# A transformer layer in float32 on one core: attention and last stage in one block, the first maxima between the projections' products, and loads spread over attention

## The chip, the core and the metric

The kernel runs on one core of one Trainium2 chip. A core has five engines that each work through a queue of their own in order and wait for each other by semaphores: TensorE (PE; its weight loads are shown as PEld), VectorE (DVE), ScalarE (ACT), GpSimd (POOL) and SyncE (SP), which here only issues DMAs (SPq in the rows). The metric is the device time of one execution in microseconds (us), the median of several.

## The reference

The layer is pre-normed attention, then a pre-normed linear map whose inputs and weights are rounded to a six bit grid, each with a residual. x is 4 x 2048 x 512, with 16 heads of 32.

```python
x = x + attn(layernorm(x))
#  q = x@Wq.T + bq + ocr_bias, k = x@Wk.T + bk, v = x@Wv.T + bv
#  scores = q k^T / sqrt(32) + 0.1 for |i-j| <= 2; softmax; (attn v) @ Wo.T + bo
x = x + ffn(layernorm(x))
#  xd, wd: x and weight in blocks of 32, scaled by max/7.5, rounded to the e2m3 grid, scaled back
#  xd @ wd.T + bias
```

## The kernel before

The 8192 tokens are 16 chunks of 512 (`NCH`; `CH` = 512 tokens, `TT` = 4 tiles of 128, `KB` = 4 blocks of the 512 features). Float32 products are made of three passes on parts: hi times hi, hi times lo, lo times hi. There are three blocks, one after the other; between two of them all engines meet, so that nothing of a later block is issued before the earlier one has ended.

**Projections** (`project`, L109). For each chunk PE turns the normed chunk (16 transposes into `ps_t`), ACT takes the high part `x_hi` (L346) and DVE the low part `x_lo` (L294), and PE makes `NP` = 12 groups of 12 products (`products`, L389 to L405) into the four banks of `ps_p`: four groups each for q, k and v. ACT and DVE take them out again as high and low parts (L354, L309) or with the bias added (v, L319), and SyncE stores them to HBM (L216, L217, L220). POOL makes `xb` = x + bo (L172). At its start ACT waits for `bias_ready` ahead of all of its first chunk. The parts of the two later weights, `wo` and `wd`, are made in the first chunk and stored.

**Attention** (`attend`, L421). A unit is one group of four heads and 512 queries (`NU` = 64 units; four units share their keys). A unit has `KT` = 16 steps s of 128 keys. In each step and for each of four heads PE makes one product of scores into `ps_s` (L644), which ACT takes out with the exponential into `p_sb` (L714); DVE multiplies by the band where it is near (L751); in each second step PE weighs the values (`weigh`, L658) and POOL adds two steps' `p_sb` to a `pair` (L798), whose sums are merged by DMAs that add, on POOL's queue (L803, `join` L784). The exponential needs each query's maximum ahead of its unit. So between the scores of a unit PE makes the products of the *next* unit (`maximum`, L625, `MAXES` = 64 for a unit) into `ps_m`, DVE reduces each to a maximum (`take`, L724), and the row of them is turned and put by a DMA (`put_shift`) into the 97th row of that unit's queries. Unit 0 has no unit ahead of it: at the head of attention PE makes 64 maxima for it and 16 (`HG * LEAD`) of unit 1, with nothing between them.

**Last stage** (`finish`, L810), for each chunk c: `load_o` loads the unscaled attention output `o_raw` and the inverted sums `o_rec`, which are rows of 512 numbers that are each spread to 32 partitions; POOL scales (L912), ACT takes `o_hi` (`o_highs`, L941), POOL makes `o_lo` (L916), PE multiplies by `wo` (`out_project`, L1054), DVE adds `xb` to get `x1` and its moments (`residual`, `norm_factors`), ACT normalises (`normalise`: `std` L930 and `y` L934), DVE quantises to `xd` (`quantise`), PE turns it and multiplies by `wd` (`linear`, L1081), and DVE adds `x1` to get `res` (`last_sum`, L1007). `last_sum(c)` is dealt out between the steps of `quantise(c + 1)`, so DVE comes to it behind the normalising of the next chunk. The FFN's bias comes in as one product of 2 rows ahead of each tile (L1073). The chunks are software-pipelined by hand. The loops that set the order are:

```python
# SyncE
for c in range(NCH):
    if c + 2 < NCH: load_xb(c + 2)
    if c + 4 < NCH: load_o(c + 4)
    store(c)
# ScalarE
for c in range(NCH):
    high(c)
    if c + 1 < NCH: normalise(c + 1)
    if c + 3 < NCH: o_highs(c + 3)
```

## Time and profile before

| | us |
|---|---|
| median of 3 runs | 4258.18 (4256.25 to 4260.35) |
| profiled execution | 4247.55, with a span of 4245.8 |
| PE busy in the span | 4096.3 (96%) |
| DVE busy | 3324.0 (78%) |
| POOL busy | 3055.4 (72%) |
| ACT busy | 2406.2 (57%) |

The page has also the span in 40 slices. PE is busy for 8 tenths or more of each of them but one, the slice from 3715 to 3821 us, where it is 4. That slice holds the border between attention and the last stage; the border between projections and attention lies around 600 us. A row of a timeline has the start, the length, the engine, the line, the work with what it writes and reads, and in brackets how long the engine had been idle ahead of it and what released it. Times in the rows are those of the profiled execution, counted from its span's start.

### The profile page before, as it was taken

Reading aid. Unit: us, or ns where it says so; the run is one execution under the profiler, and the core shown is the slowest. Engines: PE = TensorE matmul, PEld = TensorE weight load, DVE = VectorE, ACT = ScalarE, POOL = GpSimd, SP = SyncE. Lnnn points to the kernel's source line nnn. Section 1 sums busy time; section 2 is a strip of 40 time slices with the busy share of each in tenths; the row PEclk is TensorE's granted clock in tenths of the full one; section 3 lists DMA queues with packets and bytes.
Section 4 is the critical chain, followed back from the end, with each engine's and each line's share of the span. In section 5 each row is a group of like instructions: output and inputs, shape, how many; then the busy total and the mean of one; then the engine's idle time right before and its main releaser. Section 6 shows DMA issues by size and latency. Waiting matters only on the chain. (4 is left out here: it accounts for less than half of the span.)

```text
span 4245.8 us, 60060 instructions
## 1 busy us (share of the span) xinstructions
PE 4096.3 (96%) x21392; PEld 2549.3 (60%) x21392; DVE 3324.0 (78%) x5623; ACT 2406.2 (57%) x4652; POOL 3055.4 (72%) x1111
## 2 busy tenths in 40 slices
PE   8999989999999999999999999999999999949999
PEld 6888855555555555555555555555555555417777
DVE  5444449888888888888888888888888888617776
ACT  2222215766766677667666676666766677623221
POOL 2111116888889898989989889888888888935552
PEclk9999988999999999999999999999999999969999
DMA  7666655899999999999999999998999999775442
GB/s 267 207 207 207 207 173 122 182 211 190 202 197 193 201 193 208 187 206 186 212 191 196 198 192 208 186 210 184 210 190 199 195 193 188 160 185 177 160 160 72
DMA packets 283849, 808.30 MB, mean 190 GB/s; under 512 B 28609, under 2 KB 95169, under 8 KB 221122
## 3 DMA queue, kind: packets, MB, share of 16 engines
q0 software_dynamic: 64512, 469.79, 55.7%
q1 hardware_dynamic: 219074, 335.10, 27.1%
q8 instruction: 153, 2.51, 0.2%
q14 instruction: 110, 0.90, 0.1%
HBM read 195.04 MB, written 139.46 MB: 79 GB/s over the span
## 5 line engine op out<-in xcount | busy, mean ns | idle before, releaser
L724 DVE TENSOR_REDUCE part_max<-ps_m 128x1 f32<-128x512 f32 x4096 | 2512.3, 678 | 383.6 <-PE ps_m L625 383.3
L798 POOL TENSOR_TENSOR pair<-p_sb 128x2048 f32<-128x2048 f32 x512 | 2458.1, 4823 | 104.4 <-DVE p_sb L751 58.6
L714 ACT ACTIVATE p_sb<-ps_s 128x512 f32<-128x512 f32 x4096 | 2083.3, 614 | 769.6 <-PE ps_s L644 765.7
L644 PE MATMUL ps_s<-q_st,k_st 97*128 97x512 f32 x4096 | 1687.4, 413 | 6.1 <-DMA q_st<-shift 4.1
L625 PE MATMUL ps_m<-k_st,q_st 96*128 96x512 f32 x4096 | 1643.5, 405 | 20.3 <-POOL k_st L778 20.1
L644 PEld LDWEIGHTS ps_s<-q_st,k_st 97*128 97x128 f32 x4096 | 772.9, 189 | 653.8 <-issue 426.4
L658 PE MATMUL ps_o<-p_sb,v_sb 128*32 128x512 f32 x8192 | 993.4, 602 | 31.2 <-DVE p_sb L751 18.8
L625 PEld LDWEIGHTS ps_m<-k_st,q_st 96*128 96x128 f32 x4096 | 787.3, 192 | 190.9 <-DVE part_max L724 37.6
L658 PEld LDWEIGHTS ps_o<-p_sb,v_sb 128*32 128x32 f32 x8192 | 224.1, 109 | 512.2 <-ACT p_sb L714 320.9
L803 POOL DMA_DIRECT2D pair<-pair x384 | 336.2, 875 | 218.0 <-POOL pair L798 172.5
L172 POOL TENSOR_TENSOR xb<-xin,bo_row 128x2048 f32<-128x2048 f32 x16 | 73.8, 4613 | 418.3 <-DMA xin<-in_x 407.6
L751 DVE TENSOR_TENSOR p_sb<-p_sb,band_f 128x520 f32<-128x520 f32 (+2 forms) x352 | 219.1, 650 | 47.1 <-ACT p_sb L714 47.1
L309 DVE SCALAR_TENSOR_TENSOR s_lo<-ps_p,bias,s_hi 128x512 fp32r<-128x512 f32 x128 | 96.0, 750 | 172.0 <-ACT s_hi L354 172.0
L354 ACT ACTIVATE s_hi<-ps_p,bias 128x512 fp32r<-128x512 f32 x128 | 88.2, 689 | 245.5 <-PE ps_p L405 237.3
L916 POOL TENSOR_TENSOR o_lo<-o_raw,o_hi 128x512 fp32r<-128x512 f32 x60 | 128.1, 2163 | 134.3 <-ACT o_hi L941 134.3
L405 PE MATMUL ps_p<-x_hi,w_hi 128*128 128x512 f32 x512 | 203.7, 398 | 8.3 <-DVE x_lo L294 8.2
L405 PE MATMUL ps_p<-x_hi,w_lo 128*128 128x512 f32 x512 | 201.4, 393 | 0.0
L405 PE MATMUL ps_p<-x_lo,w_hi 128*128 128x512 f32 x512 | 201.0, 393 | 0.0
L1054 PE MATMUL ps_r<-wo_hi,o_hi 128*128 128x512 f32 x256 | 104.1, 406 | 39.9 <-DVE o_lo L1016 26.2
L319 DVE TENSOR_TENSOR v_st<-ps_p,bv_row 128x512 f32<-128x512 f32 x64 | 44.1, 691 | 118.5 <-PE ps_p L405 118.5
L700 ACT ACTIVATE sum_st<-ps_m 128x512 f32<-128x512 f32 x64 | 38.3, 598 | 161.8 <-PE ps_m L666 161.8
L346 ACT ACTIVATE x_hi<-ps_t 128x512 fp32r<-128x512 f32 x64 | 33.0, 602 | 160.4 <-PE ps_t L379 160.4
(98 smaller groups left out, 2685.5 us busy)
## 6 DMA issues: line engine op xcount, KB each, us to landing
pair<-pair POOLq DMA_DIRECT2D x448, 1024.0 KB, 8.6
q_st<-q_hi_d SPq DMA_DIRECT2D x128, 256.0 KB, 7.3
k_st<-k_hi_d SPq DMA_DIRECT2D x128, 256.0 KB, 12.2
xin<-in_x SPq DMA_DIRECT2D x16, 1024.0 KB, 8.3
xb_d<-xb SPq DMA_DIRECT2D x16, 1024.0 KB, 5.2
q_hi_d<-s_hi SPq DMA_DIRECT2D x64, 256.0 KB, 2.1
q_lo_d<-s_lo SPq DMA_DIRECT2D x64, 256.0 KB, 2.3
k_hi_d<-s_hi SPq DMA_DIRECT2D x64, 256.0 KB, 2.3
```

Source lines behind the costliest of these rows:

```text
L309: nc.vector.scalar_tensor_tensor(out=s_lo[:, n % RING], in0=ps_p[:, n % RING], scalar=bias[:, n // NHG, n % NHG:n % NHG + 1], in1=f32(s_hi ...
L405: last = nc.tensor.matmul(ps_p[:, n % RING], lhs, rhs, start=(k == 0 and j == 0), stop=(k == KB - 1 and j == 2))
L625: nc.tensor.matmul(ps_m[:, bank, :], q_st[0:ROWS, u, h, t * P:(t + 1) * P], k_st[0:ROWS, g % 2, n, h, :], start=True, stop=True).then_inc( ...
L644: nc.tensor.matmul(ps_s[:, (HG * s + h) % RING_S, :], k_st[0:ROWS + 1, unit // QC % 2, kt // TT, h, kt % TT * P:(kt % TT + 1) * P], q_st[0 ...
L658: last = nc.tensor.matmul(ps_o[h * HD:(h + 1) * HD, :], v_sb[:, kt, h * HD:(h + 1) * HD], p_sb[:, s % SLOTS, h, :], start=(kt == 0), stop= ...
L714: nc.scalar.activation(p_sb[:, s % SLOTS, h, :], ps_s[:, (HG * s + h) % RING_S, :], ACT.Exp, scale=SCALE).then_inc(p_ready, 1)
L724: nc.vector.tensor_reduce(part_max[:, unit % 2, col, n:n + 1], ps_m[:, max_place(unit, j) % RING_M, :], AX.X, ALU.max).then_inc(max_taken, 1)
L751: nc.vector.tensor_tensor(view, view, factor, ALU.mult).then_inc(banded, 1)
L798: nc.gpsimd.tensor_tensor(pair[:, m % PAIR_RING], p_sb[:, s % SLOTS], p_sb[:, (s + 1) % SLOTS], ALU.add).then_inc(paired, 1)
L803: pool.dma_start(pair[:, m % PAIR_RING], pair[:, (m - CHAINS) % PAIR_RING], accum_op=ALU.add).then_inc(merged[n % CHAINS], 16)
L916: nc.gpsimd.tensor_tensor(o_lo[:, b, g, :], o_raw[:, b, g, :], f32(o_hi[:, b, g, :]), ALU.subtract).then_inc(o_split, 1)
L1054: last = nc.tensor.matmul(ps_r[:, t, :], lhs, rhs, start=(k == 0 and j == 0), stop=(k == NHG - 1 and j == 2))
```

## The change

- `attend` and `finish` become one block, `attend_and_finish`; the last stage's tiles lie in buffers that attention no longer needs by then (`x1` is a ring of three in `p_sb`, and the load of `xb` goes straight into `x1`).
- The 80 first maxima and the turn of unit 0's row are made in `project`, between the groups of the last three chunks: `places(c, n)` gives 22, 22 and 37 of the 81 places to the chunks, 1 to 4 behind each group. Their products go to the banks of `ps_t`, and DVE's `take` stands behind each of its own steps. The keys and queries they need are loaded in `load_first`, behind the fifth chunk. The queries are a ring of three units instead of four.
- The loads of the last stage's first chunks and of `wo` stand between the steps of attention's last units. The output projection of chunk 0 is made between the last unit's scores (`between_scores`), DVE scales chunks 0 and 1 (`scale_o`, `o_low`).
- The FFN's bias is written to the output in the projections, 1 MB with each chunk, and the last stage's result is added to it by a DMA that adds, on POOL's queue. The product L1073 is gone.
- In the first chunk ACT waits for `bias_ready` only ahead of `s_hi`, and POOL waits for the normed chunk ahead of its first `xb`.
- The loops of the last stage load later (`load_o(c + 2)` where it was `c + 4`), in another order.

```diff
+    AHEAD = MAXES + HG * LEAD + 1
+    TURN_PLACE = MAXES + TURN_AFTER
...
+    def places(c, n):
+        ends = (0, 22, 44, AHEAD)
+        i = c - (NCH - 3)
+        count = ends[i + 1] - ends[i]
+        return range(ends[i] + count * n // NP, ends[i] + count * (n + 1) // NP)
...
+            pool.wait_ge(xhat_ready, TT)
...
+            def load_first():
+                for s in part_out:
+                    sp.wait_ge(s, 64 * QC)
+                sp.wait_ge(late_out, 64)
+                for u in range(QC):
+                    for r, part in enumerate((k_hi_d, k_lo_d, k_hi_d)):
+                        sp.dma_start(f32(k_even[r * HD:(r + 1) * HD, u]),
+                                     part[u].rearrange("(h d) t -> d h t", d=HD)).then_inc(k_loaded[u], 16)
+                for u in range(2):
+                    for r, part in enumerate((q_hi_d, q_hi_d, q_lo_d)):
+                        sp.dma_start(f32(q_st[r * HD:(r + 1) * HD, u]),
+                                     part[u].rearrange("(h d) t -> d h t", d=HD)).then_inc(q_loaded[u], 16)
...
+                if last:
+                    sp.wait_ge(max_taken, TURN_PLACE + 1)
+                    sp.dma_start(f32(q_st[ROWS:ROWS + 1, 0]).rearrange("o h (t q) -> o (h t) q", q=P),
+                                 f32(shift[:])).then_inc(shift_loaded, 16)
...
+                sp.dma_start(out_ch[c], ffn_b.unsqueeze(0).unsqueeze(0).to_broadcast([P, TT, D])).then_inc(bias_out, 16)
...
-            with sp.Fori(1, NCH - 2) as c:
+            with sp.Fori(1, QC + 1) as c:
+                chunk(c, True)
+            load_first()
+            with sp.Fori(QC + 1, NCH - 2) as c:
...
+            sp.wait_ge(bias_out, 16 * NCH)
...
+            def take(c, n):
+                for place in places(c, n):
+                    v.wait_ge(max_scored, place + 1)
...
+                    unit, j = max_of(place)
+                    n_, col = j // (HG * TT), j % (HG * TT)
+                    nc.vector.tensor_reduce(part_max[:, unit, col, n_:n_ + 1], ps_t[:, place % RING_M, :],
+                                            AX.X, ALU.max).then_inc(max_taken, 1)
+                    if place == MAXES:
+                        v.wait_ge(max_taken, MAXES)
+                        nc.vector.tensor_reduce(neg_max[:], part_max[:, 0], AX.X, ALU.max, negate=True).then_inc(max_row, 1)
...
+            def ahead(c, n):
+                for place in places(c, n):
+                    at_least(pe, max_taken, place - RING_M + 1)
+                    if place == TURN_PLACE:
+                        pe.wait_ge(max_row, 1)
+                        nc.tensor.transpose(ps_t[0:HG * TT, place % RING_M, 0:P], neg_max[:], ident[:]).then_inc(max_scored, 1)
+                        continue
...
+                    nc.tensor.matmul(ps_t[:, place % RING_M, :], q_st[0:ROWS, unit, h, t * P:(t + 1) * P],
+                                     k_even[0:ROWS, n_, h, :], start=True, stop=True).then_inc(max_scored, 1)
...
+            for c in range(NCH - 3, NCH):
+                if c > NCH - 3:
+                    pe.wait_ge(max_taken, places(c, 0)[0])
+                turn(c)
+                for n in range(NP):
+                    products(c, n)
+                    ahead(c, n)
...
+        o_first = sb("o_first", [P, NHG, CH])
+        o_hi, o_lo = (k_even[:, 0], q_st[:, 1]), (q_st[:, 2], k_odd[:, 0])
+        wo_hi, wo_lo, wd_hi, wd_lo = k_even[:, 2], k_even[:, 3], k_odd[:, 1], k_odd[:, 2]
+        t_hi, t_lo = k_odd[:, 3], q_st[:, 0]
+        x1 = (p_sb[:, 4], p_sb[:, 5], p_sb[:, 0])
...
+        res = (pair[:, 2], pair[:, 3])
...
+        def o_rec(c):
+            return pair[:, 4] if c > 1 and c % 2 == 0 else f32(k_even[:, 1])
...
+        def o_raw(c):
+            return p_sb[:, 3] if c > 1 and c % 2 == 0 else o_first
...
+            def load_o(c):
+                at_least(sp, o_split, NHG * (1 if c == 1 else c - 1))
+                sp.wait_ge(o_out, 16 * ((NHG - 1) * NCH + c + 1))
+                sp.dma_start(o_raw(c)[:], o_by_chunk[c]).then_inc(o_in[c % 2], 16)
...
+            def load_rec(c, gs=range(NHG)):
+                at_least(sp, o_scaled, NHG * (1 if c == 1 else c - 1))
...
+                for g in gs:
+                    sp.dma_start(o_rec(c)[:, g, :],
+                                 rec_d[g * NCH + c].unsqueeze(1).to_broadcast([HG, HD, CH])).then_inc(rec_in[c % 2], 16)
...
+            def load_xb(c):
+                at_least(sp, res_ready, TT * (c - 2))
+                sp.dma_start(x1[c % 3], xb_d[c]).then_inc(xb_in[c % 3], 16)
...
+                    if 0 < unit < NU - 2 and kt == 1:
+                        sp.wait_ge(scored, HG * KT * unit)
+                        load_q(unit + 2)
...
+                    if unit == NU - QC and kt == 6:
+                        sp.wait_ge(scored, HG * KT * QC * (NG - 1))
+                        sp.dma_start(f32(wo_hi), wo_hi_d).then_inc(wo_in[0], 16)
...
+                    if unit == NU - 3 and kt == 7:
+                        load_o(0)
+                    if unit == NU - 2 and kt in (2, 4, 6, 8):
+                        load_rec(0, (kt // 2 - 1,))
+                    if unit == NU - 1 and kt in (1, 2, 3, 4):
+                        load_rec(1, (kt - 1,))
+                    if unit == NU - 1 and kt == 5:
+                        load_o(1)
+                    if unit == NU - 1 and kt == KT - 1:
+                        sp.wait_ge(pv_done, ST - 4)
+                        sp.wait_ge(paired, NM - 2)
+                        load_xb(0)
+            load_xb(1)
+            sp.wait_ge(scored, HG * ST)
+            sp.dma_start(f32(wd_hi), wd_hi_d).then_inc(wd_in, 16)
+            sp.dma_start(f32(wd_lo), wd_lo_d).then_inc(wd_in, 16)
+            sp.wait_ge(pv_done, ST)
+            sp.wait_ge(paired, NM)
+            load_xb(2)
+            for c in range(NCH):
+                if c + 2 < NCH:
+                    load_o(c + 2)
+                    load_rec(c + 2)
+                if c + 3 < NCH:
+                    load_xb(c + 3)
...
+            def between_scores(kt, h):
+                t, k = (kt - FIRST_OUT) // 2, (kt - FIRST_OUT) % 2 * 2 + h // 2
+                if h % 2 == 0 or not 0 <= t < TT:
+                    return
...
+                out_part(0, t, k)
...
+                        if s >= ST - KT:
+                            between_scores(s % KT, h)
...
+            act.wait_ge(paired, NM)
+            normalise(0)
+            for c in range(NCH):
+                high(c)
+                if c + 2 < NCH:
+                    o_highs(c + 2)
+                if c + 1 < NCH:
+                    normalise(c + 1)
...
+            def last_unit(kt):
+                if kt == 3:
+                    o_low(0)
+                if kt == 9:
+                    scale_o(1)
+                if kt == 12:
+                    o_low(1)
...
             def store(c):
-                sp.wait_ge(res_ready, TT * c + TT)
-                sp.dma_start(out_ch[c], res[:, c % 2]).then_inc(out_done[c % 2], 16)
...
-            for c in range(NCH):
-                if c + 2 < NCH:
-                    load_xb(c + 2)
-                if c + 4 < NCH:
-                    load_o(c + 4)
-                store(c)
...
-            for c in range(1, NCH):
+                pool.wait_ge(res_ready, TT * c + TT)
+                pool.dma_start(out_ch[c], res[c % 2], accum_op=ALU.add).then_inc(out_done[c % 2], 16)
+            for c in range(2, NCH):
...
+                if c > 2:
+                    store(c - 3)
+            for c in range(NCH - 3, NCH):
+                store(c)
```

SyncE in the last stage, before: `out_y` is the store of a chunk, `xb2`, `o_raw` and `o_rec` are the loads for later chunks.

```order
L874 DMA out_y<-res 128x4x512 [waits res_ready]
L870 DMA xb2<-xb_d 128x2048 [waits x1_ready]
L861 DMA o_raw<-o_d 128x4x512 [waits o_split]
L865 DMA o_rec<-rec_d 128x1x512 x4
L874 DMA out_y<-res 128x4x512 [waits res_ready]
```

SyncE there now; `p_sb` and `o_first` from `o_d` are `o_raw`, `k_even` from `rec_d` is `o_rec`, and `p_sb` from `xb_d` is `x1`.

```order
L724 DMA p_sb<-xb_d 128x2048 [waits res_ready]
L710 DMA o_first<-o_d 128x4x512 [waits o_out,o_split]
L719 DMA k_even<-rec_d 128x1x512 [waits rec_out,o_scaled]
L719 DMA k_even<-rec_d 128x1x512 x3
L724 DMA p_sb<-xb_d 128x2048 [waits res_ready]
```

The load that waits for `res_ready` stands now ahead of `o_raw` and `o_rec` of the same chunk, and the store has left this queue.

ScalarE in the last stage, before, one turn of its loop.

```order
L926 ACTIVATE t_hi<-ps_t2 128x512 [waits ffn_done,turned2]
L926 ACTIVATE t_hi<-ps_t2 128x512 [waits turned2] x3
L930 ACTIVATE std2<-mom2,eps2 128x4 [waits ln2_steps]
L934 ACTIVATE y<-x1,nmr,rstd2 128x512 [waits quant,rstd2_ready]
L934 ACTIVATE y<-x1,nmr,rstd2 128x512 x3
L941 ACTIVATE o_hi2<-o_raw 128x512 [waits o_scaled,out_projected]
L941 ACTIVATE o_hi2<-o_raw 128x512 [waits o_scaled] x3
```

ScalarE there now; `k_odd` is `t_hi`, `q_st` from `o_first` is `o_hi`, `p_sb` is `y` and `x1`.

```order
L983 ACTIVATE k_odd<-ps_a 128x512 [waits ffn_done,turned2]
L983 ACTIVATE k_odd<-ps_a 128x512 [waits turned2] x3
L998 ACTIVATE q_st<-o_first 128x512 [waits o_scaled,out_projected]
L998 ACTIVATE q_st<-o_first 128x512 [waits o_scaled] x3
L987 ACTIVATE std2<-mom2,eps2 128x4 [waits ln2_steps]
L991 ACTIVATE p_sb<-p_sb,nmr,rstd2 128x512 [waits quant,rstd2_ready]
L991 ACTIVATE p_sb<-p_sb,nmr,rstd2 128x512 x3
```

The four `o_hi` stood behind `std` and `y`, and stand now ahead of them.

TensorE at the head of attention, before; the first row is the last fifteen maxima of unit 0, L631 the turn of its row, L644 the first score.

```order
L625 MATMUL ps_m<-k_st,q_st 128x512 [waits max_taken] x15
L625 MATMUL ps_m<-k_st,q_st 128x512 [waits max_taken,q_loaded1]
L625 MATMUL ps_m<-k_st,q_st 128x512 [waits max_taken] x7
L631 MATMUL ps_m<-ident,neg_max 16x128 [waits max_row,max_taken]
L625 MATMUL ps_m<-k_st,q_st 128x512 [waits max_taken] x8
L644 MATMUL ps_s<-q_st,k_st 128x512 [waits shift_loaded]
```

TensorE in the last chunk of the projections now; L489 are its products, L507 maxima of unit 0.

```order
L489 MATMUL ps_p<-x_lo,w_hi 128x512
L489 MATMUL ps_p<-x_hi,w_lo 128x512
L507 MATMUL ps_t<-k_even,q_st 128x512 [waits max_taken] x3
L489 MATMUL ps_p<-x_hi,w_hi 128x512 [waits bank_free]
L489 MATMUL ps_p<-x_lo,w_hi 128x512
L489 MATMUL ps_p<-x_hi,w_lo 128x512
```

The maxima stand between two groups of products.

## Rows read from the trace of the kernel before

**Rows 1.** Timeline of the start (start us, us, engine, line, work, [idle before]).

```profile
12.98 4.72 POOL L172 TENSOR_TENSOR xb<-xin,bo_row 128x2048 f32<-128x2048 f32 x1 [10.62 <-DMA bo_row<-in_bo]
...
13.26 4.47 DVE L324 TENSOR_TENSOR bias<-bias 128x4 f32<-128x4 f32 x1
...
22.75 0.77 PE L405 MATMUL ps_p<-x_hi,w_hi 128*128 128x512 f32 x1 [5.61 <-DVE x_lo L294]
```

**Rows 2.** Timeline of the border between projections and attention.

```profile
591.96 0.40 PE L405 MATMUL ps_p<-w_hi,x_lo 128*128 128x512 f32 x1
...
593.11 2.32 SPq L220 DMA_DIRECT2D v_d<-v_st  x4
...
598.66 1.28 ACT L714 ACT_TABLE_LOAD   x1 [16.78 <-PEq L129]
...
612.49 32.86 PE L625 MATMUL ps_m<-k_st,q_st 96*128 96x512 f32 x56 [20.14 <-POOL k_st L778]
...
659.82 0.63 PE L644 MATMUL ps_s<-q_st,k_st 97*128 97x512 f32 x1
```

**Rows 3.** Timeline of attention: PE and DVE at the maxima.

```profile
670.95 0.40 PE L625 MATMUL ps_m<-k_st,q_st 96*128 96x512 f32 x1
671.19 0.39 PE L644 MATMUL ps_s<-q_st,k_st 97*128 97x512 f32 x1
...
1501.38 4.87 DVE L724 TENSOR_REDUCE part_max<-ps_m 128x1 f32<-128x512 f32 x8
```

**Rows 4.** Timeline from attention's last pair to the first stored chunk.

```profile
3746.66 4.80 POOL L798 TENSOR_TENSOR pair<-p_sb 128x2048 f32<-128x2048 f32 x1
...
3862.97 0.68 DVE L1007 TENSOR_TENSOR res<-ps_r,x 128x512 f32<-128x512 f32 x1
```

**Rows 5.** Chain of waits in the last stage (start us, us, engine and work).

```profile
4041.48 5.45 PE ps_r L1054 x24
...
4054.56 2.95 PE ps_r L1081 x12
4057.93 2.95 PE ps_r L1081 x12
...
4067.63 5.44 PE ps_r L1054 x24
```

**Rows 6.** Timeline of the last stage: ACT and DVE.

```profile
3874.99 0.30 ACT L930 ACTIVATE std<-mom,eps 128x4 f32<-128x4 f32 x1 [8.55 <-DVE mom L102]
...
3887.26 0.68 DVE L1007 TENSOR_TENSOR res<-ps_r,x 128x512 f32<-128x512 f32 x1
...
4198.49 0.68 DVE L1007 TENSOR_TENSOR res<-ps_r,x 128x512 f32<-128x512 f32 x1
```

**Rows 7.** SyncE's store, and stretches (each engine's busy us; clock, DMA share, GB/s).

```profile
4043.29 0.38 SPq L874 DMA_DIRECT2D out_y<-res  x1
...
4052.00:4053.00 1.00, 1.00 (x6) 0.84 (x5) 0.84 (x2) 0.00 (x0) 0.00 (x0) 1.00 1.05 399
...
4055.00:4056.00 1.00, 1.00 (x6) 0.79 (x6) 0.93 (x5) 0.00 (x0) 0.00 (x0) 1.00 0.26 100
...
4063.00:4064.00 1.00, 1.00 (x6) 0.71 (x4) 1.00 (x1) 0.00 (x0) 1.00 (x2) 1.00 0.18 70
```

**Rows 8.** Timeline of chunk 2: scaling on POOL, the high part on ACT.

```profile
3838.31 5.03 POOL L912 TENSOR_TENSOR o_raw<-o_raw,o_rec 128x512 f32<-128x512 f32 x4 [11.78 <-DMA o_rec<-rec_d]
...
3843.38 0.63 ACT L941 ACTIVATE o_hi<-o_raw 128x512 fp32r<-128x512 f32 x1 [0.63 <-POOL o_raw L912]
```

**Rows 9.** Last addition, and a merge's DMA (KB each, us to landing).

```profile
4240.28 0.69 DVE L1007 TENSOR_TENSOR res<-ps_r,x 128x512 f32<-128x512 f32 x1 [2.68 <-PE ps_r L1081]
...
pair<-pair POOLq DMA_DIRECT2D x448, 1024.0 KB, 8.6
```

**Rows 10.** Stretch within the first border, columns as in Rows 7.

```profile
600.00:610.00 10.00, 0.00 (x0) 0.00 (x0) 0.00 (x0) 0.00 (x0) 10.00 (x2) 0.50 1.05 254
```

**Rows 11.** Waits of SyncE's queue (us in total, times, longest us).

```profile
SPq L554 <- DMA sum_d<-sum_st: 71.7, 15, 5.4
```

644 lines of the change are left out of this document (316 added, 328 removed).

## The prediction

> **What bounds the kernel now.** The page's slices come first: TensorE is busy everywhere but around two borders. The timeline then shows the first border. PE's last product of the projections starts at 591.96, SyncE stores v at 593.11, the block ends at 598.66, and the first of the unguarded maxima starts only at 612.49, when the queries, the keys and the row of ones are there; the first score, with which attention proper begins, starts at 659.82 [rows 2]. So 659.82 - 592.36 = 67.5 us lie between the last product and the first score. The second border is as plain: the last pair of attention starts on POOL at 3746.66 for 4.80, and the first finished chunk of the last stage ends at 3862.97 + 0.68 = 3863.65 [rows 4]. Behind it the chain of waits is TensorE alone: a turn of the loop takes 4067.63 - 4041.48 = 26.15 us, and no row of it waits for a load [rows 5]. From the first finished chunk (3863.65) to the fourteenth (4198.49 + 0.68 = 4199.17) it is 335.5 us, 25.8 for each of 13 [rows 4, 6]. The rest of the last stage is 4245.8 - 4199.2 = 46.6.
>
> **The start.** ACT no longer waits for the bias before it takes the weights' high part. DVE's addition of four numbers of bias took 4.47 us, all of it beside POOL's addition of 4.72, and the first product started at 22.75 [rows 1]. That wait goes out of the path, which saves at most the 4.47. I take 3, between 0 and 6. The Trainium skill's page "SBUF — State Buffer" (SBUF: two separate sides) states that a DVE instruction with two SBUF inputs and a GpSimd one lock each other out for their whole length, and the long addition agrees. By that rule the split of the weights, which DVE now does next, can be locked out in its place, and the gain would be nearer to 1 or 2 than to 3.
>
> **The first border.** The 81 places cost PE 671.19 - 670.95 = 0.24 us each in attention, where scores and maxima alternate at full clock [rows 3]; 81 x 0.24 = 19.4. DVE needs 4.87 / 8 = 0.61 for each [rows 3], and it has room between its own steps, as only 1 to 4 maxima stand behind a group of products. Where it hasn't (each of two chunks has to wait until its last maximum is taken before it may turn the next one), PE waits; I take 5 us in all, between 0 and the 81 x 0.61 - 19.4 = 30 by which DVE alone would be slower. The end of the block stays: 598.66 - 592.36 = 6.3, and behind the stores of v comes now the last MB of bias, 4.1 us at the 254 GB/s that the loads there had [rows 10], between 0 and 10.5 (at 100 GB/s, the slowest stretch of rows 7). Behind the block the first score can start at once. Its clock is no loss: PE was at the lower of its two levels (a granted clock of 0.50) through the pause before [rows 10], and it still was at the first score, whose row is 0.63 long against 0.39 [rows 2, 3]. So 67.5 - 19.4 - 5 - 6.3 - 4.1 = **32.7 saved**. The loads of load_first lie in the projections, behind chunk 4, with eight chunks before they are needed; I cost them at nothing, and a few us if they hold up the stores of that chunk. The same holds for the bias of each chunk.
>
> **The second border.** The loads of wo, o_raw and o_rec and the output projection of chunk 0 go under attention's last units. The 48 products of chunk 0 come at 5.45 / 24 = 0.23 each [rows 5], 10.9 us, into the last unit, in which DVE makes no maxima and the pairs on POOL set the pace; I take 4 of them as added, between 0 and 10.9. What comes then is a chain of its own. Pair ends at 3751.5 + 4 = 3755.5; its merge lands 8.6 later [rows 9], and only then may o_rec of chunk 2 be loaded into its buffer: 1.05 MB at 100 GB/s [rows 7] with 1.1 ahead of it, 11.6; POOL's scaling until ACT's last high part, 3844.01 - 3838.31 = 5.7 [rows 8]; and from std to the last addition of the chunk before, 3887.94 - 3874.99 = 12.95 [rows 6]. Sum 3794.3. I take 3795 for the first finished chunk: 3863.65 - 3795 = **68.6 saved**, between 45 and 75.
>
> **The last stage's loop.** It loses the product for the bias. A tile of the linear map goes by in 4057.93 - 4054.56 = 3.37, its 12 products in 12 x 0.227 = 2.72 [rows 5], so the bias costs 0.65, 2.6 in a turn. If PE stayed the bound, a turn would take 23.55. I don't think it does, for the new order closes a ring. Follow the order of instructions on SyncE and ScalarE. x1 of chunk c + 3 lies where x1 of chunk c was, so its load waits for the last addition of chunk c. In SyncE's queue o_raw and o_rec of chunk c + 3 stand behind it. POOL needs them to scale. ACT takes chunk c + 3's high parts *before* it makes std and y of chunk c + 2. And DVE makes the last addition of chunk c + 1 between the steps of the quantising that needs that y. So from one chunk's last addition to the next one's there are:
> - the loads. Before, a store of 1 MB, xb, o_raw and o_rec went out together at 4043.29 and were in at about 4063.7: 20.4. DMA was full at 399 GB/s in the stretch at 4052, and from 4053 to 4063.7 it was a tail at a share of 0.26 and 100 GB/s [rows 7]. That tail is o_rec, 1.05 MB. Without the store (0.4 to issue, 1.05 MB / 399 = 2.6) it is 17.4;
> - POOL and ACT, 5.7 [rows 8];
> - std to the last addition, 12.95 [rows 6]; some semaphores, 0.2.
>
> Together **36.2** against 25.8. The ring holds 13 times (chunks 3 to 15 are loaded so): 13 x (36.2 - 25.8) = **135.2 lost**. The load takes at least 16.8 (1.1, 2.1 MB at 399, the tail) and at most, in a batch that is no larger than before, 20.4: turns of 35.6 to 39.2. Once, the last sums' store and load stand in the same queue; SyncE waited 71.7 / 15 = 4.8 for such a store [rows 11], 4.8 lost. Before, the ring wasn't there: o_raw was loaded four chunks ahead of the loop, and ACT took the high parts behind y.
>
> The Trainium skill's page "DMA: Bandwidth & Descriptors" (Why a DMA increments its semaphore by 16 and not by 1) states that a DMA is dealt to the largest number of engines up to 16 that divides the slowest dimension of both sides, here the 4 rows of o_rec. The tail's share, 0.26 of 16, agrees. Were o_rec dealt to all 16 at 399 GB/s, its tail would be 2.6 in place of 10.5, a turn 28.3 and the loss 33.
>
> **The end.** The last two chunks lose 2 x 2.6 of bias. The last addition ended at 4240.97, 4.8 before the end; an adding DMA of 1 MB takes 8.6 to land [rows 9] and 0.9 to issue, 4.7 more. Sum 0.5 saved.
>
> **Sum.** -3 - 32.7 - 68.6 + 135.2 + 4.8 - 0.5 = +35.2 against the profiled execution's span of 4245.8, 0.83%. That execution took 4247.55, 10.6 under the median; I put the 35 on the median: 4258 + 35 = **4293**.
>
> **The rivals.**
> - *The ring doesn't bind* (I misread an order, or the loads are in much sooner). Then PE stays the bound: 13 x (23.55 - 25.8) = -29.3 in place of +140, in all -134: 4124. It would be the faster side. For it speaks that PE works without a pause now; against it the four orders above, each of which is in the code.
> - *The ring binds, but shorter.* The balance is even at a turn of 25.8 + 100 / 13 = 33.5, that is at a load of 14.7. With the 9.5 of an o_rec on 16 engines the time would be 4191. The tail at 100 GB/s in rows 7 speaks against it.
> - *The adding stores fall into the loads.* A chunk's store stands on POOL behind the low parts of three chunks later, about 31 us into a turn of 36, and its 8.6 us reach into the next turn's loads. Were that 5 us a turn, 65 more: 4358. No row shows an adding DMA to HBM.
> - *The maxima hold the projections up*, DVE alone setting the pace: 25 us less saved, 4318. Its other steps leave it half of each chunk, so this is a matter of the range.
>
> **How the numbers follow.** Chances: the ring at about 36, 0.68; no ring, 0.12; a shorter ring, 0.08 (0.05 of it faster); stores in the loads, 0.12. About 0.2% (8.5 us) is what a measurement of this kernel can tell from no change. Faster 0.12 + 0.05, within 0.07, slower 0.76. The bounds of the forecast's own terms (turns of 35.6 to 39.2, borders 25 worse or 15 better) give 4270 to 4350; the range goes to 4250 for the shorter ring and to 4350, which leaves out the case without a ring and the longest ones.
>
> **What would show it.** Right: PE idle in each turn of the last stage, with DVE's rstd or ACT's o_hi waiting for POOL's scaling and that for o_rec; turns near 36 between finished chunks; the first score at about 659.8 - 3 - 32.7 = 624; the first chunk finished at 3863.7 - 3 - 32.7 - 68.6 = 3759 and the fourteenth at 3759 + 13 x 36.2 + 4.8 = 4235. Wrong: a last stage whose chain is TensorE alone, with turns of 23 to 24.

## The result and the profile after

The changed kernel takes **4358.65 us** (median of 4 runs, 4355.95 to 4362.84) against 4259.27 for the kernel before on the same chip (4256.25 to 4261.27): a ratio of 1.0235, 95% interval 1.0217 to 1.0253. It is slower by about 99 us. The forecast was 4293 with a range of 4250 to 4350: the sign and the mechanism in the last stage were right, the size was not. The profiled execution has a span of 4354.2 us against 4245.8 before, 108.4 more.

The page of the changed kernel (busy time of TensorE, then three of its rows in 40 slices of 109 us, then the chain that ended last, by engine):

```profile
PE 4061.6 (93%) x21328; PEld 2558.6 (59%) x21328; DVE 3330.7 (76%) x5630; ACT 2409.8 (55%) x4651; POOL 3006.1 (69%) x1118
...
PE   7989989999999999999999999999999999767776
...
PEclk9999999999999999999999999999999999888888
DMA  7788758999999999999999999999999998734444
...
PE 55%; DVE 14%; DMA 7%; ACT 3%; POOL 3%; issue 2%; SPq 1%; POOLq 0%; ACTq 0%
```

TensorE now has room in the last six slices, at a granted clock of 0.8, and there is a dent at the third slice, inside the projections. DMA, of which no last-stage chain spoke before [rows 5], holds 7% of the chain.

**The last stage** first, since the largest term of the forecast stands there. One turn of its loop in the chain of waits of the changed kernel (start us, us, what), from one chunk's last addition to the next one's:

```profile
3975.81 0.69 DVE pair L1118
...
3976.51 0.33 SPq L724
...
3976.95 0.38 SPq L710
...
3977.45 0.53 SPq L719
...
3979.71 15.06 DMA k_even<-rec_d
...
3994.92 4.93 POOL o_first L1224 x4
...
4000.41 0.29 ACT std L987
...
4008.32 1.28 DVE pair L1118 x2
4009.61 1.27 DVE p_sb L1087
...
4011.72 0.69 DVE pair L1118
```

That is the ring of the forecast, row by row: the last addition lets SyncE issue the load of x1 (L724), behind it stand o_raw (L710) and o_rec (L719); POOL scales; ACT makes std after its last high part; DVE makes the last addition. The loads take 3994.81 - 3976.51 = 18.3 (forecast 17.4), POOL and ACT 5.6 (5.7), std to the last addition 12.0 (12.95): 35.9 together, in one of the shortest turns (most are 36.4 to 37.3). No TensorE row is in it.

**The borders** are where the time of the forecast didn't come. The timeline of ACT in the changed kernel, at the first step of chunks 0, 1, 2, 5, 6, 14 and 15 of the projections (before, chunk 0 took 41.7 and each of the others 35.4):

```profile
14.61 0.60 ACT L429 ACTIVATE x_hi<-ps_t 128x512 fp32r<-128x512 f32 x1 [1.63 <-PE ps_t L463]
...
64.13 2.07 ACT L429 ACTIVATE x_hi<-ps_t 128x512 fp32r<-128x512 f32 x4 [6.80 <-PE ps_t L463]
...
104.51 2.06 ACT L429 ACTIVATE x_hi<-ps_t 128x512 fp32r<-128x512 f32 x4 [10.45 <-PE ps_t L463]
...
211.09 2.07 ACT L429 ACTIVATE x_hi<-ps_t 128x512 fp32r<-128x512 f32 x4 [11.03 <-PE ps_t L463]
...
265.30 2.07 ACT L429 ACTIVATE x_hi<-ps_t 128x512 fp32r<-128x512 f32 x4 [11.19 <-PE ps_t L463]
...
555.53 2.07 ACT L429 ACTIVATE x_hi<-ps_t 128x512 fp32r<-128x512 f32 x4 [15.10 <-PE ps_t L463]
...
597.89 2.06 ACT L429 ACTIVATE x_hi<-ps_t 128x512 fp32r<-128x512 f32 x4 [15.02 <-PE ps_t L463]
```

Chunk 5 takes 265.30 - 211.09 = 54.2 instead of 35.4. What happened in it (SyncE's queue, a stretch, and ACT):

```profile
213.80 0.74 SPq L281 DMA_DIRECT2D out_y<-in_ffn_b  x1
214.90 0.53 SPq L252 DMA_DIRECT2D k_even<-k_hi_d  x1
...
231.09 1.03 SPq L256 DMA_DIRECT2D q_st<-q_lo_d  x1
232.49 0.67 SPq L271 DMA_DIRECT2D q_hi_d<-s_hi  x1
```

```profile
236.00:252.00 16.00, 0.89 (x2) 0.80 (x3) 1.13 (x2) 1.38 (x2) 0.00 (x0) 0.59 1.04 269
```

```profile
249.59 0.69 ACT L439 ACTIVATE s_hi<-ps_p,bias 128x512 fp32r<-128x512 f32 x1 [24.92 <-DMA q_lo_d<-s_lo]
```

The columns of the stretch are those of [rows 7]. The bias store and 18 loads of load_first stand in the queue ahead of chunk 5's first store of queries, DMA is at a share of 1.04, and ACT waits 24.92 us for a store to land before it may use its staging again. That wait has two parts. SyncE alone takes from 213.80 to 232.12 to issue the bias store and the 18 loads, one after the other, and only then comes to a store whose data has lain ready since about 217; and this chunk's stores of queries then land after 14.2 to 14.6 us (median) instead of 6 to 7. TensorE computes for 0.89 of the 16 us.

The end of the block and the first score of attention, which answer [rows 2]:

```profile
640.32 1.07 PE L507 MATMUL ps_t<-k_even,q_st 96*128 96x512 f32 x4
655.38 0.76 PE L845 MATMUL ps_a<-q_st,k_even 97*128 97x512 f32 x1 [13.98 <-PEq L164]
```

The last unit, which answers [rows 4]: DVE's scaling of chunk 1, the pair on POOL behind the bands that stand behind it, the last pair, and the last addition of chunk 0.

```profile
3746.18 2.50 DVE L1124 TENSOR_TENSOR o_first<-o_first,k_even 128x512 f32<-128x512 f32 x4 [36.58 <-DMA o_first<-o_d]
```

```profile
3752.12 4.90 POOL L1202 TENSOR_TENSOR pair<-p_sb 128x2048 f32<-128x2048 f32 x1 [15.35 <-DVE p_sb L1063]
...
3766.84 4.72 POOL L1202 TENSOR_TENSOR pair<-p_sb 128x2048 f32<-128x2048 f32 x1
```

```profile
3826.88 0.68 DVE L1118 TENSOR_TENSOR pair<-ps_b,p_sb 128x512 f32<-128x512 f32 x1
```

Between them lies this piece of the chain of waits:

```profile
3709.63 36.53 DMA o_first<-o_d
...
3772.11 14.28 DMA pair<-pair
...
3795.85 14.06 DMA pair<-rec_d
...
3810.08 4.93 POOL p_sb L1224 x4
```

Three transfers hold the chain for 36.5, 14.3 and 14.1 us: a load of 1 MB, a merge of 1 MB, and the last quarter of a load of o_rec, from its issue on. The forecast had the first at nothing and the merge at 8.6 [rows 9].

The first is not slow just because it runs beside the merges. The same load for chunk 0, issued at 3611.99, runs beside them too. These are the DMA rows of the two (KB, us to landing), chunk 0's first and then chunk 1's, and what SyncE issued just ahead of chunk 1's:

```profile
o_first<-o_d SPq DMA_DIRECT2D x1, 1024.0 KB, 7.9
o_first<-o_d SPq DMA_DIRECT2D x1, 1024.0 KB, 36.5
```

```profile
3697.66 2.73 SPq L719 DMA_DIRECT2D k_even<-rec_d  x3
3700.61 1.18 SPq L691 DMA_DIRECT2D o_d<-o_st  x1
3701.88 7.40 SPq L719 DMA_DIRECT2D k_even<-rec_d  x1
3709.63 4.58 SPq L710 DMA_DIRECT2D o_first<-o_d  x1
```

The four loads of o_rec of chunk 1 (L719), each on a quarter of the engines, leave SyncE in the 12 us just ahead of it; chunk 0's were issued 30 us behind its o_raw. The store of 256 KB among them took 20.5 us to land, where the same store took 7 to 8 before. So the loads of o_rec ahead of it in the queue are the likelier cause. No run moves them: the new cut of e3 leaves chunk 1 as it was.

### The profile page after: what moved, and what is told of

The parts are those of the page before. It is cut to its first block, busy times and chain, and to the rows that moved or that the text cites. A ratio compares the mean times of both kernels' runs of the same rounds, so it can differ in the third digit from the quotient of the medians.

```text
span 4354.2 us, 59922 instructions
## 1 busy us (share of the span) xinstructions
PE 4061.6 (93%) x21328; PEld 2558.6 (59%) x21328; DVE 3330.7 (76%) x5630; ACT 2409.8 (55%) x4651; POOL 3006.1 (69%) x1118
## 4 chain that ended last, share of the span: by engine, by line
PE 55%; DVE 14%; DMA 7%; ACT 3%; POOL 3%; issue 2%; SPq 1%; POOLq 0%; ACTq 0%
PE ps_a L859 19%; PE ps_a L845 19%; PE ps_b L824 16%; DVE part_max L1036 8%; DVE p_sb L1063 3%; DMA k_even<-rec_d 2%; ACT p_sb L1012 2%; DMA pair<-rec_d 2%; PE ps_b L870 1%; SPq L719 1%; DVE pair L1118 1%; POOL pair L1202 1%; DMA o_first<-o_d 1%; POOL o_first L1224 1%; POOL p_sb L1224 1%
## 5 line engine op out<-in xcount | busy, mean ns | idle before, releaser
L1036 DVE TENSOR_REDUCE part_max<-ps_b 128x1 f32<-128x512 f32 x4016 | 2464.1, 678 | 368.2 <-PE ps_b L824 368.0
L1012 ACT ACTIVATE p_sb<-ps_a 128x512 f32<-128x512 f32 x4096 | 2084.0, 616 | 713.9 <-PE ps_a L845 709.9
L859 PE MATMUL ps_a<-p_sb,v_sb 128*32 128x512 f32 x8192 | 990.0, 600 | 34.3 <-DVE p_sb L1063 22.9
L845 PE MATMUL ps_a<-q_st,k_odd 97*128 97x512 f32 x2048 | 844.7, 415 | 18.4 <-ACT p_sb L1012 16.6
L845 PE MATMUL ps_a<-q_st,k_even 97*128 97x512 f32 x2048 | 844.4, 412 | 15.4 <-PEq L164 14.0
L824 PE MATMUL ps_b<-k_odd,q_st 96*128 96x512 f32 x2048 | 813.3, 397 | 0.0
L824 PE MATMUL ps_b<-k_even,q_st 96*128 96x512 f32 x1968 | 782.7, 398 | 0.0
L845 PEld LDWEIGHTS ps_a<-q_st,k_odd 97*128 97x128 f32 x2048 | 388.3, 190 | 342.8 <-issue 212.9
L845 PEld LDWEIGHTS ps_a<-q_st,k_even 97*128 97x128 f32 x2048 | 387.6, 189 | 330.7 <-issue 228.2
L824 PEld LDWEIGHTS ps_b<-k_odd,q_st 96*128 96x128 f32 x2048 | 389.2, 190 | 75.7 <-DVE part_max L1036 8.8
L489 PE MATMUL ps_p<-x_hi,w_hi 128*128 128x512 f32 x512 | 203.3, 397 | 3.4 <-DVE x_lo L373 3.0
L489 PE MATMUL ps_p<-x_hi,w_lo 128*128 128x512 f32 x512 | 201.1, 393 | 0.0
L489 PE MATMUL ps_p<-x_lo,w_hi 128*128 128x512 f32 x512 | 200.8, 392 | 0.0
```

Of the source, the lines that this page charges most:

```text
L489: last = nc.tensor.matmul(ps_p[:, n % RING], lhs, rhs, start=(k == 0 and j == 0), stop=(k == KB - 1 and j == 2))
L824: nc.tensor.matmul(ps_m[:, bank, :], q_st[0:ROWS, unit % RING_Q, h, t * P:(t + 1) * P], k_st[g % 2][0:ROWS, n, h, :], start=True, stop=Tru ...
L845: nc.tensor.matmul(ps_s[:, (HG * s + h) % RING_S, :], k_st[unit // QC % 2][0:ROWS + 1, kt // TT, h, kt % TT * P:(kt % TT + 1) * P], q_st[0 ...
L859: last = nc.tensor.matmul(ps_a[h * HD:(h + 1) * HD, RING_S, :], v_sb[:, kt, h * HD:(h + 1) * HD], p_sb[:, s % SLOTS, h, :], start=(kt == 0 ...
L1012: nc.scalar.activation(p_sb[:, s % SLOTS, h, :], ps_s[:, (HG * s + h) % RING_S, :], ACT.Exp, scale=SCALE).then_inc(p_ready, 1)
L1036: nc.vector.tensor_reduce(part_max[:, unit % 2, col, n:n + 1], ps_m[:, max_place(unit, j) % RING_M, :], AX.X, ALU.max).then_inc(max_taken, 1)
```

## The experiments

All are edits of the changed kernel, and are compared with its 4358.65. The kernel before, run again beside them, took 4254 to 4256, and 4259.27 beside the changed kernel; so some 5 us between two medians are no effect of an edit, and the small gains below rest on the rows of the traces. Turns are the times between the last additions of successive chunks, first to fourteenth, a thirteenth of the sum.

### The ring, cut at its three places

**e1: SyncE's order.** The load of x1, which waits for a last addition, goes behind the loads of o_raw and o_rec.

```
-                if c + 3 < NCH:
-                    load_xb(c + 3)
+                if 3 <= c + 2 < NCH:
+                    load_xb(c + 2)
```

> Only the order in SyncE's queue is changed: the load of x1 for chunk c + 3 no longer stands ahead of the loads of o_raw and o_rec for that chunk, but behind them. Theory (a ring through that wait holds the last stage at 36.9 us a turn): the ring is open, the loads leave most of a turn earlier, and TensorE is the bound again, 23.6 a turn. 13 x (36.9 - 23.6) = 173 less: 4359 - 173 = 4186. Rival (the loads are slow for themselves, beside the adding stores: 3 MB in and 1 MB added per turn, of which o_rec alone takes 10.5 on a quarter of the engines): turns of 30 or more, so 4270 or more. Rival (the order on ScalarE holds the stage, not the one on SyncE): turns stay at 36 to 37, 4359.

Measured: **4199.23** (4195.39 to 4203.45), 159 less where 173 was expected; a ratio to the kernel before of 0.9867 (0.985 to 0.9883). Turns of 24.9 instead of 36.9. The ring is what held the stage, and exchanging two lines of queue order is enough to open it. The rival by which the loads are slow for themselves falls. The turns alternate, 21.3 and mostly 28 to 29 long. In the long ones VectorE's and GpSimd's work fall on one another; from the chain of waits of e1, two operations on 4 numbers a partition and the scaling back on VectorE:

```profile
4014.80 1.26 DVE mom L111
4016.06 1.28 DVE mom L112
```

```profile
3978.40 3.35 DVE p_sb L1087
```

In the changed kernel the same rows are 0.16 and 2.28 long on average. Both have two inputs in SBUF, and GpSimd is scaling or splitting at the time. The Trainium skill's page "SBUF — State Buffer" (Who interferes with whom) states that a VectorE instruction with two SBUF inputs contends with a GpSimd instruction that reads SBUF; the rows agree, but no run here takes GpSimd's work away to show it.

**e2: ScalarE's order.** std and y of chunk c + 1 go back ahead of the high parts of chunk c + 2.

```
-                if c + 2 < NCH:
-                    o_highs(c + 2)
                 if c + 1 < NCH:
                     normalise(c + 1)
+                if c + 2 < NCH:
+                    o_highs(c + 2)
```

> Only ScalarE's order is changed: std and y of chunk c + 1 come ahead of the high parts of o of chunk c + 2, as in the kernel before; SyncE's order is left. Theory of the ring: the path from the wait for a last addition to the loads (18), the scaling and splitting (10) and TensorE's output projection, turns and linear map of that chunk's neighbour (26) is now 54 long but goes round once in two turns, so 27 a turn: 13 x (36.9 - 27) = 129 less, 4230. Rival (only the late load matters, wherever the high parts stand): turns stay near 36, 4350. Rival (TensorE is the bound at once): 23.6 a turn, 4186.

Measured: **4289.78** (4288.03 to 4296.74), 69 less where 129 was expected. The turns alternate as a ring that goes round once in two turns must: 37.0, 28.7, 36.4, 29.1 and so on, 32.8 on average. So it is a ring of 65 us instead of the 54 I had worked out. The chain of waits of e2 tells where the 11 lie:

```profile
4006.53 20.37 DMA k_even<-rec_d
...
4027.04 7.10 POOL o_first L1224 x4
```

The loads take 4026.9 - 4002.4 = 24.5 instead of 18, and the scaling 7.1 instead of 4.93; from the last split to the last addition it is 4067.0 - 4038.7 = 28.4. The shape of the theory holds, and my rows for its parts, taken from the other order, were too short.

**e3: o_rec on all DMA engines.** The ring stays closed; the same bytes are loaded by head instead of by group (chunks 2 to 15).

```
+                    for h in range(HG):
+                        sp.dma_start(o_rec(c)[h * HD:(h + 1) * HD],
+                                     rec_by_chunk[c, h].unsqueeze(0).to_broadcast([HD, NHG, CH]))
```

> The ring is left closed. Only the four loads of o_rec of a chunk (from chunk 2 on) are cut another way: one for each head, 32 partitions by 4 groups, instead of one for each group, 4 heads by 32 repeated rows. The bytes are the same. Theory (the tail of 10.5 us at a quarter of the engines stands in the ring in full): spread over all engines it takes 2.6, a turn shrinks by 7.9 to 29.0, 13 x 7.9 = 103 less: 4256. Rival (the tail is the reading of repeated rows from HBM, however it is dealt out): no change, 4359. Rival (other traffic fills the room, the adding stores above all): 3 us a turn, 4320.

Measured: **4285.3** (4277.3 to 4287.13), 73 less where 103 was expected, with turns of 31.5. The loads of a turn take 3991.3 - 3977.7 = 13.6 instead of 18.3. Of each profile the last stretch of those loads (columns as in [rows 7]), the changed kernel's and then e3's:

```profile
3988.00:3994.80 6.80, 6.80 (x32) 5.51 (x30) 0.00 (x0) 0.00 (x0) 0.00 (x0) 1.00 0.23 89
```

```profile
3987.00:3991.30 4.30, 4.30 (x20) 3.48 (x20) 0.38 (x3) 0.00 (x0) 0.00 (x0) 1.00 0.66 132
```

The share of the DMA engines at the end of the load goes from 0.23 to 0.66. So the tail was in good part a matter of how many engines the DMA is dealt to. The Trainium skill's page "DMA: Bandwidth & Descriptors" (Why a DMA increments its semaphore by 16 and not by 1) states that the slowest dimension of the two sides sets how many engines a DMA gets, up to 16. The rise in the share agrees with it. The rival by which the cut changes nothing falls. But the rate doesn't rise to 399. The stretch of e3 takes in the end of the load, when the engines run dry; two of its microseconds with all engines busy are

```profile
3987.00:3989.00 2.00, 2.00 (x10) 1.60 (x10) 0.38 (x3) 0.00 (x0) 0.00 (x0) 1.00 1.07 217
```

217 GB/s at a share of 1.07, against 100 at 0.26 in the changed kernel from 3988 to 3992. So each engine moves about half as much as in the old cut (an estimate: 217 / 1.07 against 100 / 0.26), and a quarter of the engines was not the whole of it. Why isn't shown; that repeated rows read from all engines are slow is left open.

**e8: both orders.**

> SyncE's order of e1 and ScalarE's order of e2 together. In e2 the first finished chunk came at 3806 instead of 3828, as std and y of chunk 1 no longer stood behind the high parts of chunk 2, which wait for the late load of o_rec; in e1 a turn took 24.8. Theory (the two effects lie behind one another): 4199 - 22 = 4177. Rival (with the ring open, the 22 us are waited for by something else, TensorE's output projection of chunk 2 above all, which needs that load too): 4199 to 4190.

Measured: **4236.99** (4232.85 to 4244.3). Neither was right: the two edits together are 38 *slower* than e1 alone. The first finished chunk comes at 3814.8 instead of 3828.3, but the turns are 28.4 instead of 24.9. In e8 GpSimd's split waits until ScalarE has made y, and then stands in the path beside VectorE's quantising. Its row in the timeline of e8, and the same kind of row in that of e1:

```profile
4011.11 9.23 POOL L1228 TENSOR_TENSOR k_odd<-o_first,q_st 128x512 fp32r<-128x512 f32 x4 [11.28 <-ACT q_st L998]
```

```profile
3985.14 5.06 POOL L1228 TENSOR_TENSOR k_odd<-o_first,q_st 128x512 fp32r<-128x512 f32 x4 [2.25 <-ACT q_st L998]
```

9.23 us against 5.06 for one instruction group, and the chain of waits of e8 has it in every turn (POOL L1228 holds 38% of it from 3993 to 4048). So ScalarE's new order, one of the four links of the ring, is a gain once the ring is open at SyncE. This I had not seen. How much of the 3.4 us a turn is the longer split and how much the later start, no run separates.

### The first border

**e4: the first loads spread.** Of the 18 loads of load_first three go ahead of each of chunks 5 to 10.

```
-            load_first()
-            with sp.Fori(QC + 1, NCH - 2) as c:
-                chunk(c, True)
+            for i in range(QC + 2):
+                load_first(i)
+                chunk(QC + 1 + i, True)
+            with sp.Fori(2 * QC + 3, NCH - 2) as c:
+                chunk(c, True)
```

> The ring is left closed. Only the 18 loads of the first queries and keys, 4.7 MB, are changed: 3 of them ahead of each of chunks 5 to 10 of the projections instead of all 18 ahead of chunk 5. Theory (they held up chunk 5's stores for 18.8 us because they stood in SyncE's queue at once): the projections' chunk 5 is back at 35.4, and 0.8 MB more per chunk are hidden: 15 to 19 less, 4342. Rival (the bytes are what costs, since the projections leave the DMA engines little room): most of the 18.8 comes back over six chunks, 4352 to 4359.

Measured: **4341.56** (4336.69 to 4345.53), 17 less, as the theory has it. Chunk 5 is back at 35.4 (209.55 to 244.93) and the first score comes at 634.9. The bytes cost nothing when they are spread; standing all at once in one queue ahead of a store that has to land costs.

**e6: other places for the bias stores.** None in chunks 0, 14 and 15, two each in 11 to 13.

```
-                sp.dma_start(out_ch[c], ffn_b.unsqueeze(0).unsqueeze(0).to_broadcast([P, TT, D]))
+                for i in fill:
+                    sp.dma_start(out_ch[c + i], ffn_b.unsqueeze(0).unsqueeze(0).to_broadcast([P, TT, D]))
```

> Only the places of the 16 stores that fill the output with the bias are changed: none in chunks 0, 14 and 15 of the projections, one in each of chunks 1 to 10, two in each of chunks 11 to 13. Theory (the store of chunk 0 held up the stores of queries and keys behind it by 3 and 5 us, and the one of chunk 15 the end of the block by 4): 10 to 12 less, 4348. Rival (the start is late through the other stores and loads there, the weights' above all, and the end through the stores of v): 0 to 4 less, 4355 to 4359.

Measured: **4358.19** (4348.53 to 4364.98), no difference. In the trace both are true: chunk 1 takes 35.8 instead of 40.4, and the way from chunk 15's first step to the first score 48.9 instead of 57.5; but the chunks that follow two stores (12 to 14) take 40.2, 47.5 and 45.2 instead of 35.4, 42.4 and 42.4, and chunk 0 took 54.4 instead of 49.5 in this execution. (That last is not the edit's: over the executions looked at, chunk 0 takes 49 to 54.) The loss moved with the stores.

**e10: without the bias.** The stores of the bias are left out, and the result is stored instead of added; the linear map's bias is missing from the output.

```
-                sp.dma_start(out_ch[c], ffn_b.unsqueeze(0).unsqueeze(0).to_broadcast([P, TT, D]))
...
-                pool.dma_start(out_ch[c], res[c % 2], accum_op=ALU.add).then_inc(out_done[c % 2], 16)
+                pool.dma_start(out_ch[c], res[c % 2]).then_inc(out_done[c % 2], 16)
```

> The bias of the linear map is left out: no stores of it in the projections, and the result is stored plainly instead of added to what lies in HBM; the ring stays closed. Theory (the ring is made of the loads, the scaling and std to the last addition; the adding stores lie beside it): turns stay at 36.9, the end is 3 to 5 shorter, and the projections get back 4 at the end of the block and at most 5 in chunk 1: about 4348. Rival of the forecast (each adding store falls into the loads of the next turn): 5 us a turn less, 4285.

Measured: **4325.36** (4323.93 to 4327.7), 33 less, three times what I expected. The turns are 36.7: the rival by which the adding stores fall into the loads is out. The end, last addition to the end of the span, is 6.2 instead of 10.4. The rest is in the projections: the first score at 632.2 instead of 655.4, of which chunk 1 gives 5.0, chunk 5 11.0 and the end of the block 8.6. On the page, the DMAs of the queries' stores (KB each, median us from issue to landing) in the changed kernel:

```profile
q_hi_d<-s_hi SPq DMA_DIRECT2D x64, 256.0 KB, 6.2
q_lo_d<-s_lo SPq DMA_DIRECT2D x64, 256.0 KB, 7.2
```

and without the bias stores:

```profile
q_hi_d<-s_hi SPq DMA_DIRECT2D x64, 256.0 KB, 2.0
q_lo_d<-s_lo SPq DMA_DIRECT2D x64, 256.0 KB, 2.3
```

Each store of 1 MB of bias stands ahead of the next chunk's first stores, and in the median the stores of queries land 4 to 5 us later with it. In most chunks nobody waits for that; in three places somebody does. The stall of chunk 5 is bias and first loads together: without the one 43.2, without the other 35.4, with both 54.2.

### The second border

**e5: chunk 1's splitting on GpSimd**, behind attention's last pair instead of on VectorE inside the last unit.

```
-                if kt == 9:
-                    scale_o(1)
-                if kt == 12:
-                    o_low(1)
...
-            for c in range(2, NCH):
+            for c in range(1, NCH):
```

> Ring, loads and stores of the projections are as in the changed kernel. Chunk 1's scaling, high parts and low parts are taken out of attention's last unit: GpSimd does the scaling and the low parts behind its last pair (the join of the two chains of sums comes behind them), ScalarE the high parts behind std and y of chunk 0. Theory (VectorE stood still for 36.6 us in the last unit for the load of o_raw of chunk 1, and the bands, the pairs and TensorE behind it): the last pair starts some 17 us earlier and the first finished chunk with it: 4359 - 17 = 4342. Rival (the work only moves: the output projection of chunk 1 now waits for GpSimd, and o_rec of chunk 2 is still loaded behind it): 0 to 5 less, 4354 to 4359.

Measured: **4347.36** (4337.8 to 4353.37), 11 less. In the trace the last unit, from its row of shifts to its last pair, takes 64.1 instead of 78.3 us, and the first finished chunk comes 13.4 earlier, though this execution's first score came 4.3 later. Chunk 1's splitting on VectorE was what held the pairs, and in the trace its wait for o_raw is 36.58 us of it. In all eight traces in which VectorE scales chunk 1 within the last unit, that stretch takes 78 to 79 us; in the five without, 60 to 64; in the kernel before, 58.1.

### Putting it together

**e7: all of it**, with ScalarE's order of e2.

> All of it together: both orders, o_rec dealt to all DMA engines, the first loads spread over six chunks, the bias stores off the first and the last chunks, chunk 1's splitting on GpSimd. If the terms add: 4177 - 17 (first loads) - 10 (bias) - 17 (last unit) - 8 (one shorter load of o_rec on the path at the border, nothing in the turns) = 4125. If they share their gains at the second border (the load of o_rec for chunk 2 and the merges of the last unit end at one time whatever the rest does): 4177 - 27 - 0 to 10, about 4145.

Measured: **4195.26** (4193.21 to 4204.41), far from both: turns of 27.8. It carries e8's order on ScalarE; e9, without that order (and without e6's places for the bias, which gained nothing), has 23.7. The first finished chunk comes at 3780.

**e9: e1, e3, e4 and e5**, ScalarE's order as in the changed kernel.

> SyncE's new order of e1 (ring open), with ScalarE's order left as in the changed kernel, and besides it o_rec on all DMA engines, the first loads spread over six chunks, and chunk 1's splitting on GpSimd. If the gains add: 4199 - 17 (first loads) - 13 (last unit) - 8 (one shorter o_rec on the path at the border) = 4161. Turns of about 25, since TensorE is the bound in them. Rival (the second border hides one of the gains): 4175.

Measured: **4157.48** (4151.96 to 4160.07); ratio to the kernel before 0.9767 (0.975 to 0.9784). The sum held within 4 us. Its turns are 23.7 long, and its chain of waits from 3916 to 3990 has nothing in it but TensorE's products:

```profile
by line: PE ps_b L899 47.2%; PE ps_b L946 44.9%; PE ps_a L929 8.1%
```

**e12: e9 with the old loads of o_rec.**

> e9 without the new cut of o_rec's loads (they are on a quarter of the engines again). Theory (with the ring open the loads leave most of a turn early, so a tail of 10 us costs nothing in the turns, and 8 once at the second border): 8 more than e9. Rival (GpSimd's scaling, which starts when the load is in, falls beside other work of VectorE at a later time, and both slow down): 20 or more above e9.

Measured: **4164.7** (4159.04 to 4171.23), 7 more than e9 (the intervals just touch), about as forecast, yet by another way: the turns are 24.4 on average and mostly alternate again (21.3 and 28.4), as in e1. So the longer tail costs 13 x 0.76 = 10 us in the loop of this trace. Its borders were no worse than those of e9.

**e11: e9, and the stores of the split weights two each behind chunks 1 and 2.**

```
+            late = ((wd_hi_d, wd_hi), (wd_lo_d, wd_lo), (wo_hi_d, wo_hi), (wo_lo_d, wo_lo))
+            for c in range(1, QC + 1):
+                chunk(c, True)
+                for d, w in late[2 * c - 2:2 * c]:
+                    sp.dma_start(d, f32(w)).then_inc(late_out, 16)
```

> e9 with one more edit: the four stores of the split weights, 4 MB in all, don't stand behind chunk 0 in SyncE's queue but two each behind chunks 1 and 2. Theory (chunk 1 starts its queries late because its first stores stand behind 5 MB of weights and bias): chunk 1 is 5 shorter and the others unchanged: 5 less than e9. Rival (DMA is full through the first three chunks, and the loss only moves): no difference from e9.

Measured: **4147.61** (4146.94 to 4155.82); ratio to the kernel before 0.9745 (0.9729 to 0.9761). Chunk 1 takes 35.4 instead of 38.6, and the first score comes at 633.9. The median is 10 under e9's, but the intervals overlap and the two profiled spans are 4154.0 and 4154.6, so only the 3 us in chunk 1 are shown. They tell something of the changed kernel too: chunk 1 is back at 35.4 with its bias store in place, as it is in e10 with the stores of the weights in place. It takes both ahead of chunk 1 to hold it up. e11 is the version with the lowest median, 2.5% under the kernel before and 4.8% under the changed one.

## Why the prediction was right or wrong

Forecast and measured, as differences to the span before (4245.8):

| step | forecast | measured | from |
|---|---|---|---|
| first score (659.82 before) | -35.7 | -4.4 | 655.38 |
| first finished chunk (3863.65) | -104.3 | -36.1 | 3827.56 |
| fourteenth finished chunk (4199.17) | +35.7 | +107.6 | 4306.79 |
| end (4245.8) | +35.2 | +108.4 | 4354.2 |

**Where the 73 us lie.** The execution ended 108.4 later where 35.2 was forecast. Of the 73 us between them 31.3 are lost by the first score, 36.9 from there to the first finished chunk, 3.8 in the thirteen turns and 1.3 behind them.

**The start: right, and worth nothing.** ScalarE's first step came at 14.61 instead of 19.58, 5 earlier where 3 was forecast. But chunk 0 then took 49.5 instead of 41.7. ScalarE stands still in it for 7.27 us until VectorE has made the moments of chunk 1, where it did for 2.61 before, and for 5.20 until a store of queries has landed (3.09 before). VectorE in its turn waited for chunk 1's x, which SyncE issued at 20.51, 0.5 us ahead of 1 MB of the linear map's weight; and that weight and the first stores of queries (at 22.08, where it was 28.85) now stand close behind it. That the saved time is lost again because steps that come earlier meet loads that don't is argued from these rows; no run undid it. It isn't the bias: e10 has 49.4.

**The first border: the step that failed.** The terms that the forecast had written down nearly held. The maxima cost 7.0 + 7.0 + 8.6 = 22.6 (forecast 19.4 + 5). The end of the block took 14.0 from the last maximum to the first score (10.4); e10 gives the bias store there 8.6, where the forecast had 4.1. What failed is the sentence that costed the loads of load_first at nothing, "and a few us if they hold up the stores of that chunk", and "the same holds for the bias of each chunk". They cost 18.8 in chunk 5 (e4 has that chunk back at 35.4, and is 17 faster) and, with the stores of the weights, 5.0 in chunk 1. With the 7.8 that chunk 0 lost, for which nothing was set down either, that is 31.6, and the first score came 31.3 late. I had looked at how many bytes were to be moved and by when they were needed, eight chunks later. I had not asked what stands *behind* them in the queue, and who waits for that to land.

**The second border: mis-sized in three terms.** From first score to first finished chunk the forecast missed by 37:
- The last unit was 16.1 longer than its 58.1 + 4. I had taken only the 48 products as its price, and the loads at nothing, as at the first border. o_raw of chunk 1 is loaded there into a buffer that is free only after chunk 0's low part, behind four loads of o_rec, and needed 36.5 us where such a load takes 8 in the last stage. VectorE stands in order behind it, the bands behind VectorE, the pairs behind the bands. e5 shows that chunk 1's splitting in this place costs the time; why the load took 36.5 is argued above.
- The last merge took 14.9 to land instead of 8.6 [rows 9], 6.3 more, and the load of o_rec behind it 23.6 instead of 11.6, 12.0 more. Loads of x1, of the weights and of o_raw are in flight at the same time. e3 and e5 bear on it only partly, and the split of these 18 us isn't settled.
- Attention's other units were 4.5 longer. Over fourteen traces that stretch varies by up to 16 us without a pattern that I can name, so this is left open.

**The ring: right.** Turns of 36.86 with the sums' store among them (36.68 without) where 36.2 was forecast; all thirteen turns and the store cost 479.2 against 475.4. Each of its parts is within 1 us of its row, since each was a row of the kernel before at the same work. e1 shows that it is closed through SyncE's order, and e2 and e3 that ScalarE's order and the tail of o_rec set its length, as the forecast has it.

**The end: right.** Last addition to the end 10.4 (forecast 9.5), and the bias product of the last chunks gone, 4.8 (5.2).

**The rivals.** *Without a ring* a turn would have taken 23.55: e9, with the ring open and the tail gone, has 23.66, and e1 24.9. *A shorter ring* is e3. *The adding stores in the loads* gave 4358, which is the measured time, for a reason that e10 refutes: without them a turn is 36.7. The number was hit by chance. *Maxima held up by DVE* is refuted by the 22.6.

**The range.** Its upper end allowed "borders 25 worse". They were 68 worse. The bounds came from the terms that I had written down; edits costed at nothing had no upper bound in it, and these made the miss. The sum of the bounds was wrong as well: 25 for the borders and 13 x 3.0 for turns of 39.2 give 4293 + 64 = 4357, not 4350. And the 100 GB/s that the forecast calls the slowest stretch of rows 7 isn't: the last one there has 70.

## What to carry to other kernels

An in-order DMA queue has two lists to be gone through when a transfer is put into it: what it waits for, and what now stands behind it and must *land* for somebody to go on; "it is needed much later" says nothing about the second. A load that waits for the result of turn c must not stand ahead of loads that don't: here the exchange of two lines was worth 159 us. And a step that is put into an engine's full loop is only as harmless as the load it waits for, since all that stands behind it in order waits too; e5 put it on another engine, behind the loop, and the last unit was 14 us shorter.
